# The values product of a self-attention step, in two halves of 256 queries behind the two pairs of score matmuls

## What is computed

```python
# layer 0
out = merge(softmax(Q K^T / 4) V) + x                 # Q from x, K and V from the context
# layer 1
qn = layernorm(x);  q, k, v = split(qn @ sa_in_w.T + sa_in_b)
x = x + merge(softmax(q k^T / 4) v) @ sa_out_w.T + sa_out_b        # self-attention over 1024 tokens
xn = layernorm(x);  x = x + attention(xn, ctx) @ co_w.T + co_b     # cross-attention, 77 keys
xn = layernorm(x);  x = x + gelu(xn @ w1.T + b1) @ w2.T + b2
```

## Time and profile before

| | before |
|---|---|
| median of 3 runs, us | 836.05 (835.07 to 841.61) |
| the profiled execution's span, us | 836.5 |
| PE busy | 749.0 us, 90% |
| DVE busy | 530.3 us, 63% |
| ACT busy | 452.1 us, 54% |
| POOL busy | 164.8 us, 20% |
| DMA moved | 52.82 MB |

### The profile page before, as it was taken

The page is one execution under the profiler, slowest core; times in us unless marked ns, Lnnn a source line. Parts: engine busy times, 40 slices in busy tenths (PEclk is TensorE's granted clock), DMA queues, the critical chain, the costliest instruction groups (busy, mean ns, idle before and its releaser), DMA issues.

```text
span 836.5 us, 11551 instructions
## 1 busy us (share of the span) xinstructions
PE 749.0 (90%) x4182; PEld 338.4 (40%) x4224; DVE 530.3 (63%) x836; ACT 452.1 (54%) x826; POOL 164.8 (20%) x355
## 2 busy tenths in 40 slices
PE   6677896589999999999999999997989897999998
PEld 3333444235222222222333333332444453556767
DVE  3445978475888888888878878874457767140001
ACT  4355553245776777777666666666644645422120
POOL 7312362364000000000000101223123214030000
PEclk9779899698999999999999999999999999999999
DMA  8967515992014060511406001004261730000001
GB/s 268 187 176 130 124 41 147 120 163 74 2 23 56 1 77 2 64 15 24 54 1 77 2 2 23 20 21 90 48 155 48 143 45 2 1 1 25 26 13 38
DMA packets 43769, 52.82 MB, mean 63 GB/s; under 512 B 9344, under 2 KB 29760, under 8 KB 43712
## 3 DMA queue, kind: packets, MB, share of 16 engines
q1 hardware_dynamic: 43424, 51.99, 32.7%
q10 hardware_dynamic: 288, 0.08, 0.1%
HBM read 36.31 MB, written 15.15 MB: 62 GB/s over the span
## 4 chain that ended last, share of the span: by engine, by line
PE 72%; DMA 11%; DVE 7%; ACT 4%; issue 3%; SPq 2%; POOL 1%; another core or an unknown queue 0%; ACTq 0%; DVEq 0%; POOLq 0%
PE PV L742 18%; PE ST L728 15%; PE SM L675 12%; PE ST L641 5%; PE ST L637 5%; DMA stacks<-mrow 3%; DMA stacks<-q_parts 3%; DVE nm L949 3%; PE SM L628 3%; PE SM L618 2%; DMA q_parts<-split 2%; PE SM L622 2%; PE PV L641 2%; PE PV L637 2%; PE SM L680 2%
## 5 line engine op out<-in xcount | busy, mean ns | idle before, releaser
L843 ACT ACTIVATE prob<-ST 128x512 f32<-128x512 f32 (+1 forms) x640 | 346.2, 598 | 180.9 <-PE ST L728 152.0
L949 DVE TENSOR_REDUCE nm<-SM 128x1 f32<-128x1024 f32 x256 | 303.0, 1220 | 65.4 <-PE SM L675 64.2
L728 PE MATMUL ST<-stacks 128*128 128x512 bf16 (+1 forms) x598 | 204.7, 391 | 20.7 <-DMA stacks<-mrow 13.9
L742 PE MATMUL PV<-prob,Vst 128*32 128x512 f32 x1280 | 174.8, 619 | 3.1 <-ACT prob L843 2.8
L675 PE MATMUL SM<-stacks 96*128 96x512 bf16 x512 | 153.2, 383 | 23.0 <-DMA stacks<-q_parts 14.3
L728 PEld LDWEIGHTS ST<-stacks 128*128 128x128 bf16 (+1 forms) x640 | 57.1, 101 | 206.6 <-ACT prob L843 141.7
L952 DVE TENSOR_REDUCE nm<-SM 128x4 f32<-128x308 f32 x128 | 58.3, 473 | 47.9 <-PE SM L680 47.2
L675 PEld LDWEIGHTS SM<-stacks 96*128 96x128 bf16 x512 | 47.9, 98 | 80.6 <-DVE nm L949 20.1
L1116 POOL CAST mp<-nm 128x16 bf16<-128x16 f32 x48 | 9.6, 199 | 356.3 <-DVE nm L949 249.2
L905 DVE TENSOR_TENSOR X<-ST,X 128x256 f32<-128x256 f32 x18 | 7.5, 423 | 90.5 <-PE ST L641 73.7
L742 PEld LDWEIGHTS PV<-prob,Vst 128*32 128x32 f32 x1280 | 25.5, 109 | 62.8 <-ACT prob L843 34.7
(11 more groups left out here) (102 smaller groups left out, 674.3 us busy)
## 6 DMA issues: line engine op xcount, KB each, us to landing
stacks<-q_parts SPq DMA_DIRECT2D x144, 128.0 KB, 5.7
q_parts<-split SPq DMA_DIRECT2D x24, 384.0 KB, 4.3
stacks<-k_parts SPq DMA_DIRECT2D x48, 128.0 KB, 7.5
k_parts<-split SPq DMA_DIRECT2D x8, 384.0 KB, 3.8
fm<-in_xT SPq DMA_DIRECT2D x4, 512.0 KB, 7.9
X<-in_x SPq DMA_DIRECT2D x4, 512.0 KB, 5.2
V<-in_w SPq DMA_DIRECT2D x2, 1024.0 KB, 9.0
out<-X SPq DMA_DIRECT2D x16, 128.0 KB, 1.7
```

The lines of the kernel that those rows point to most:

```text
L728: mm(ST[0:att.keys, n % 3, :], keys_of(att, g, h, kt), QST[att.name][g % att.buffers][:, h, j * BLK:(j + 1) * BLK], start=True, stop=True) \
L742: last = mm(PV[h * 32:(h + 1) * 32, :], Vst[:, g % 2, kt, h, :], prob[:, t % 2, h, :], start=(kt == 0), stop=(kt == att.kt - 1))
L843: act_fn(prob[0:att.keys, t % 2, h, :], ST[0:att.keys, n % 3, :], ACT.Exp) \
L949: ins = vec.tensor_reduce(nm[:, q % 2, v // QUAD, v % QUAD:v % QUAD + 1], ps, AX.X, ALU.max, negate=True)
```

## The change

For an attention with `whole` (only `A1`), `values` is called twice in a step: behind h = 1 for the queries 0 to 255, behind h = 3 for the queries 256 to 511, each time behind the side work of that slot. The waits stand at the first half, `pv_done` is incremented by the last matmul of the second. The `start` flag of a query block is set in its first half only. The last step of the attention (t = 128) has both halves without scores. For `A0` and `A2` the call stays as it was. Types, weights and all other orders stay.

```diff
-                def values(t):
+                def values(t, first, count):
                     q, kt = divmod(t, att.kt)
                     g = q // HALVES
-                    if kt == 0:
+                    if kt == 0 and first == 0:
                         pe.wait_ge(vst_ready, att.g0 + g + 1)
                         if att.q0 + q >= 1:
                             pe.wait_ge(pv_out, att.q0 + q)
-                    pe.wait_ge(exp_done, (att.t0 + t + 1) * QUAD)
+                    if first == 0:
+                        pe.wait_ge(exp_done, (att.t0 + t + 1) * QUAD)
+                    queries = slice(first, first + count)
                     for h in range(QUAD):
-                        last = mm(PV[h * 32:(h + 1) * 32, :], Vst[:, g % 2, kt, h, :], prob[:, t % 2, h, :],
-                                  start=(kt == 0), stop=(kt == att.kt - 1))
-                    last.then_inc(pv_done, 1)
+                        last = mm(PV[h * 32:(h + 1) * 32, queries], Vst[:, g % 2, kt, h, :], prob[:, t % 2, h, queries],
+                                  start=(kt == 0 and first == 0), stop=(kt == att.kt - 1 and first + count == BLK))
+                    if first + count == BLK:
+                        last.then_inc(pv_done, 1)
...
-                        if h == 1 and 1 <= t <= att.steps:
-                            values(t - 1)
+                        if h == 1 and not att.whole and 1 <= t <= att.steps:
+                            values(t - 1, 0, BLK)
+                        if h % 2 and att.whole and 1 <= t <= att.steps:
+                            values(t - 1, h // 2 * BLK // 2, BLK // 2)
```

## The result

| | before | after |
|---|---|---|
| median, us (4 runs each, side by side) | 835.56 (831.06 to 841.61) | 868.82 (867.27 to 870.04) |
| ratio, 95% interval | | 1.0381 [1.0332, 1.0430] |
| span of the profiled execution, us | 836.5 | 868.2 |
| first to last values block of A1, us | 410.6 | 444.6 |

The kernel is 3.8% slower, 33 us; 863 were forecast, in a range of 850 to 877. Both halves of the table tell the same: A1 takes 34.0 us more. The stretch ahead of A1 was 3.3 us shorter in this execution and the one behind it 1.0 longer; both lie within what the traces of all kernels here show, none of which changes anything there (198.4 to 204.5 us ahead, 222.0 to 226.0 behind).

A forecast was written before the change was run, and what follows sets the result against it. TensorE, without a real gap in an ordinary step, was taken as the bound. Ordinary steps +20.0, query-block changes +9.4, corrections -1.4, -0.3 and -1.0 gave +26.7 us, so 863 us, range 850 to 877.

The forecast's parts named there:

- The price of a second block: Ordinary A1 step on TensorE: two half blocks with entering and leaving cost 1.33 us against 1.095, extra 0.235 us.
- the new wait: ScalarE's first exponential of a step waits for the second half through pv_done; claimed to cost nothing in an ordinary step.
- The change of query block, first interval: Every eighth step: ScalarE's copy of PV waits for the second half and delays the third exponential, +1.06 us.
- the two with statistics: Two changes of query block with VectorE's statistics: first interval from 3.75 to 4.09 us, +0.34 and not +1.06.
- The second interval: Interval after the copy at a change of query block: the max's bank wait behind the transposes goes, -0.39 us.
- The two steps with the normalization: Two steps where VectorE also normalizes stay bound by it and take less than their 0.235 us: -0.3 us.
- The tail: End of A1, max units used up: steps 0.36 us shorter in four, two losing it to a stack wait; -1.0 us.
- The sum: All of A1: 20.0 + 9.4 - 1.4 - 0.3 - 1.0 = +26.7 us.
- (a): Rival: each half block's second pass is held by its weight loads, +24 us, about 888 us; chance 0.09.
- upper bound: Extra per ordinary step if the second pass starts no sooner than 0.45 us after the first: 0.45 us.
- (b): Rival: entering and leaving narrow blocks costs nothing extra, so 836 us, no change; chance 0.06.
- (c): Rival: the block's 1.00 us is a wait on ScalarE, not stream; -0.285 us a step, about 804 us; chance 0.03.

The follow-up runs named there:

- the adjacent halves: Changed kernel with both half blocks of values one behind the other behind h = 1: 838.69 us, ratio 1.0013 against the kernel before.
- the quarters: Changed kernel with four separate values blocks of 128 queries per step, around the side work of h = 1 and h = 3: 933.83 us.
- the transposes moved: Kernel before, with A1's output transposes behind h = 2 instead of h = 3 and its max unit: 830.58 us, ratio 0.9908.

## Why the prediction was right, point by point

**The price of a second block** was 0.235 a step, measured 0.247 as the mean over the 83 ordinary intervals (+20.5 us, where 19.5 had been put down for them). The half block is 0.57, the quarter 0.35, both as computed; what is missing is 0.01 for entering. The reason given, that TensorE pays for each change between bf16 matmuls on the full array and f32 matmuls on 32 columns, is shown by the adjacent halves (no price) and the quarters (0.49 for two more). In the values blocks width and type change at once, but other steps of the kernel before tell them apart. Steps with f32 products of full width:

```profile
486.14 1.06 PE L742 MATMUL PV<-prob,Vst 128*32 128x512 f32 x8
...
489.84 1.06 PE L742 MATMUL PV<-prob,Vst 128*32 128x512 f32 x8
...
526.73 1.07 PE L742 MATMUL PV<-prob,Vst 128*32 128x512 f32 x8
...
531.28 1.07 PE L742 MATMUL PV<-prob,Vst 128*32 128x512 f32 x8
```

The first has the four records of line 628 more than an ordinary step of 2.83 and takes 3.70, the second the four of line 618 and takes 4.55: 0.87 and 1.72 more, which is what their columns alone need (4 x 0.217 and 4 x 0.43). So f32 between bf16 matmuls costs nothing extra at full width, while the bf16 transposes of line 688, with 12 columns in the stationary operand, cost 0.21 more than their columns. It is the narrow operand and not the type that is paid for. The draining that the Trainium skill names ("TensorEngine Tiling (Array Packing)", Key Properties) fits this, with 0.245 us a block as its measured size. The 60 cycles that the same page of the Trainium skill (Instruction Overhead) gives for each matmul don't show as an addition: eight more adjacent records cost 0.01 us, and the measurement decides.

**That the new wait doesn't bite in an ordinary step** held: ScalarE waits for the score, as in the time line above.

**The change of query block, first interval:** +1.06 was forecast, +1.11 measured (12 intervals), +0.38 in each of the two with statistics, forecast +0.34. The copy as its cause is shown by the run that moves it: the whole term is gone.

**The second interval** was the first mis-sized term. -0.39 in each of 14 was forecast, -5.5 us; -0.37 came in eight of them, -0.28 in two and -0.02 to +0.03 in four, together -3.5. In those six a side product stands in the same step (line 628 in the two, 622 or 618 in the four), and its read on VectorE releases the transposes, before the change as after it. One of the four:

```profile
530.46 0.81 DVE L895 TENSOR_SCALAR fm<-SM,cols 128x512 f32<-128x512 f32 x1
530.48 0.60 PE L675 MATMUL SM<-stacks 96*128 96x512 bf16 x2
...
531.32 0.42 PEld L694 LDWEIGHTS SM<-ident,pvT 128*128 128x128 f32 x4 [0.75 <-DVE fm L895]
```

This is after; the kernel before has the same 0.75. The mistake was to take one change of query block for all fourteen.

**The two steps with the normalization** stayed as long as they were (4.35), +0.0 where -0.3 against the ordinary price had been put down, which is +0.2.

**The tail** was the second: -1.0 forecast, +2.9 measured in the 14 intervals from the 114th block on. The relief in steps without max units is there (2.56 to 2.21 in two of the four, forecast 2.20, and to 2.14 in a third), but I had left out a fifteenth change of query block, +1.04. Four more steps paid their 0.25. And two intervals around the wait for the stack of A2 grew by 1.09 and 0.66. TensorE idles 3.94 us for that stack where it idled 3.54, and the granted clock is down behind it for twice as long. The first line is the kernel before, the others are after:

```profile
586.30:589.70 3.40, 3.40 (x24) 1.19 (x20) 0.68 (x2) 1.83 (x5) 0.00 (x0) 0.50 0.98 120
...
613.40:620.20 6.80, 5.92 (x44) 2.24 (x45) 1.91 (x4) 2.88 (x5) 0.09 (x1) 0.50 0.53 67
...
609.00:614.00 5.00, 1.06 (x12) 0.34 (x12) 0.31 (x1) 1.30 (x3) 0.00 (x0) 0.94 0.97 134
614.00:619.30 5.30, 4.97 (x36) 1.90 (x37) 1.38 (x3) 2.28 (x4) 0.00 (x0) 0.50 0.57 72
619.30:645.00 25.70, 24.04 (x226) 11.01 (x227) 10.37 (x28) 17.50 (x32) 3.45 (x14) 0.98 0.22 33
```

(stretch in us, then busy PE, PEld, DVE, ACT, POOL, then the granted clock, DMA share and GB/s). After 1.06 us of work in 5.0 us the clock is 0.50, so 1.2 GHz, for 6.8 us, and the first two half blocks there last 1.01 each; before, it was 0.50 for 3.4 us. How much of the 1.09 and 0.66 belongs to the change is open: the interval with the wait was 6.38 before, 6.54 with the transposes moved and 8.11 with the adjacent halves, neither of which has a second separate block in a step.

**The sum:** 20.5 + 13.4 + 0.8 - 3.5 + 0.0 = 31.1 (the terms are rounded) up to the 114th block, forecast 27.7, and +2.9 behind it, 34.0 in all where 26.7 were forecast. The terms are of the forecast's kind, the two mis-sized ones make 6 of the 7 us by which it fell short in A1.

**The rivals:** second passes held by their loads (a) fell with the result, whose half block is 0.57 long and not 0.785, and for shorter passes with the quarters. The prediction had priced this rival too low: a step has two half blocks, so it would have cost another 0.43 a step and not 0.215, 49 us and not 24, and its upper bound of the extra was 0.665 and not 0.45. The forecast itself doesn't use that figure, only the end of the range leans on it. No price at all (b) fell with the result, and holds where the halves are adjacent. A block that is a wait on ScalarE (c) fell with the result too: it wanted a half block of 0.31.

## What to carry to other kernels

Where one engine is full, count how often it changes between full and narrow stationary operands, not only the work: splitting a block of narrow matmuls was free as long as its halves stayed together, and cost 0.245 us for each further place it was put. Before splitting work to let others breathe, ask which wait it is to cure and cure that by order: here one side unit moved by one slot made most changes of query block 0.62 us shorter and gave 0.9%. And work that copies a sum out has to move along with the place where the sum is complete, or all that is queued behind it waits too.

## What I had not expected of the hardware

A pass of 128 columns in the values block, where four matmuls lie side by side, costs no more than its columns: two passes, leaving included, take 0.35 us, and 16 records put in one row take 1.01 us against 1.00 for eight. Full-width f32 matmuls between bf16 ones cost their columns alone, 0.87 us for four records of 256. And moving a 1.00 us block by two scores and one max unit cost 26 us in 128 steps without one instruction more: 17.7 because the copy of the finished sum then held up the exponentials, and 8.3 that stay with the copy moved as well.
